# A landmark-attention stage with four 32-row score tiles in one PSUM buffer, half of its softmax tiles left unnormalised, and its residual loads ahead of the expert weights

## What is computed

```python
kernel1 = softmax(einsum('bhnd,bhmd->bhnm', Q, K_l), axis=-1)   # 16 heads, 64 landmarks
SV = matmul(matmul(kernel1, iterative_inv(kernel2)), matmul(kernel3, V))
out = SV @ w_proj                                                # added to the residual
```

## Time and profile before

| | us |
|---|---|
| median of 3 runs | 2002.76 (2001.23 to 2005.08) |
| the profiled execution | 2008.18 |
| its span in the trace | 2006.5 |
| kernel1 in it | 1517.05 to 1673.47 |

### The profile page before, as it was taken

One profiled execution on the slowest core, in us unless ns is written; L12 is line 12 of the kernel. 1 busy time (PEld: TensorE's weight loads), 2 busy tenths in 40 slices (PEclk: granted clock), 3 DMA queues, 4 the chain that ended last, 5 costly groups with the idle time before them and its releaser, 6 DMA issues. The chain is left out here.

```text
span 2006.5 us, 34424 instructions
## 1 busy us (share of the span) xinstructions
PE 1745.2 (87%) x11935; PEld 926.1 (46%) x12021; DVE 1530.2 (76%) x3643; ACT 1015.0 (51%) x1941; POOL 538.1 (27%) x623
## 2 busy tenths in 40 slices
PE   0898946889999999999999978978677888999998
PEld 0465621223232323232323235645575657888854
DVE  7997649988988989898999938678566994444456
ACT  3464422566767676767676835357413544232210
POOL 0343243000000000000151010045405884666610
PEclk9999976999999999999999988998787999999999
DMA  3466575005040505050551155122215224666566
GB/s 105 152 199 220 186 193 117 1 2 162 2 163 2 162 3 162 3 148 17 153 139 52 43 183 173 64 80 90 95 46 203 97 94 124 192 186 191 166 227 218
DMA packets 162940, 241.33 MB, mean 120 GB/s; under 512 B 21939, under 2 KB 131507, under 8 KB 161107
## 3 DMA queue, kind: packets, MB, share of 16 engines
q1 hardware_dynamic: 126930, 155.08, 25.9%
q0 software_dynamic: 23136, 75.65, 10.7%
q10 hardware_dynamic: 12704, 8.39, 1.4%
HBM read 118.86 MB, written 119.82 MB: 119 GB/s over the span
## 5 line engine op out<-in xcount | busy, mean ns | idle before, releaser
L1118 ACT ACTIVATE c_prob<-c_pst 128x512 f32<-128x512 f32 (+1 forms) x1152 | 578.8, 578 | 301.5 <-PE c_pst L1083 122.9
L1226 DVE TENSOR_REDUCE c_mx<-c_pf 128x2 f32<-128x1024 f32 x384 | 459.4, 1221 | 35.2 <-PE c_pf L1060 31.9
L1079 PE MATMUL c_pst<-c_qa,c_ka 128*128 128x512 bf16 (+3 forms) x1194 | 339.2, 355 | 14.4 <-DMA c_qa<-c_mT 5.8
L1095 PE MATMUL c_po<-c_prob,c_vh 128*32 128x512 f32 (+3 forms) x2560 | 295.7, 544 | 1.0 <-ACT c_prob L1118 0.4
L1060 PE MATMUL c_pf<-c_ka,c_qa 64*128 64x512 bf16 (+3 forms) x1280 | 230.1, 367 | 50.3 <-DMA c_ka<-s_kbias 22.5
L1222 DVE CUSTOM_DVE_ANT_0 c_spare<-c_pf,c_cut 128x384 f32<-128x384 f32 (+3 forms) x512 | 230.8, 491 | 28.6 <-PE c_pf L1060 24.3
L1079 PEld LDWEIGHTS c_pst<-c_qa,c_ka 128*128 128x128 bf16 x1280 | 110.2, 97 | 202.8 <-ACT c_prob L1118 110.1
L1060 PEld LDWEIGHTS c_pf<-c_ka,c_qa 64*128 64x128 bf16 x1280 | 59.4, 93 | 311.7 <-DVE c_mx L1226 122.2
L992 POOL IOTA c_zero<- 128x24 int32 x6 | 1.3, 214 | 632.3 <-PE c_po L1095 632.3
L2218 POOL DMA_INDIRECT s_parts<-x_yr,x_tags x144 | 140.4, 975 | 85.5 <-DVE x_yr L2867 62.8
L2852 DVE TENSOR_TENSOR x_h<-x_ps,x_sg 128x256 f32<-128x256 f32 x72 | 30.6, 425 | 142.0 <-ACT x_sg L2821 142.0
(11 more groups left out here) (440 smaller groups left out, 3027.1 us busy)
## 6 DMA issues: line engine op xcount, KB each, us to landing
s_slots<-c_zero POOLq DMA_DIRECT2D x6, 3264.0 KB, 17.0
x_xr<-s_slots SPq DMA_DIRECT2D x72, 272.0 KB, 2.8
x_rows<-s_parts SPq DMA_DIRECT2D x8, 2048.0 KB, 8.9
c_qa<-s_qs SPq DMA_DIRECT2D x64, 192.0 KB, 7.3
c_ka<-s_ks SPq DMA_DIRECT2D x64, 192.0 KB, 7.5
s_qs<-b_parts SPq DMA_DIRECT2D x32, 256.0 KB, 2.4
s_ks<-b_parts SPq DMA_DIRECT2D x32, 256.0 KB, 2.7
s_vs<-b_va SPq DMA_DIRECT2D x32, 256.0 KB, 3.8
```

Of the source, the lines that this page charges most:

```text
L1079: mm = nc.tensor.matmul(pst[:, u % NS, at:at + qn], ka[:, s, hh, kt * P:(kt + 1) * P], qa[:, s, hh, qb * QB + q0:qb * QB + q0 + qn], start ...
L1095: mm = nc.tensor.matmul(po[HV * h:HV * h + HV, q0:q0 + qn], vh[:, s, kt, h, :], prob[:, a % NP, h, at:at + qn], start=(kt == 0), stop=(a i ...
L1118: nc.scalar.activation(prob[:, g % NP, hh, 0:w], pst[:, u % NS, 0:w], ACT.Exp).then_inc(exp_ok, 1)
L1226: nc.vector.tensor_reduce(mx[:, fh:fh + 2, qt, part], pf[:, slot, :, 0:kn], AX.X, ALU.max).then_inc(max_ok, 1)
```

## The change

Scores. They are now made in four tiles of 32 rows (two heads each) instead of two of 64 rows, so a step takes 8 products of 128 columns instead of 4 of 256. The four tiles write four PSUM banks, half of each, and there is one such buffer instead of two: scores of step n wait for the shift of step n - 1. On TensorE scores move behind values in a round.

Odd steps (batch 1). Their exponentials are not summed on VectorE nor normalised on GpSimd. k_e is turned as it is, values multiplies it with W and, with 8 further products, with a tile of ones, which gives each head's sum on every one of that head's 16 rows. A new part on VectorE, invert, takes the reciprocal of those 128 x 256 sums (k_ss), and a new part on GpSimd, scale, multiplies k_svt with it before the projection. Even steps keep sums and normalise.

Loads. SP now issues one residual tile, then one piece of the weights, and so on, where the residual tile of step n waits for the add of step n - 2; all ten weight pieces stand behind the first ten residual tiles.

Start. Head mask and identity are kept from an earlier stage instead of being made again (in the experts stage too); each of the four kbd products signals by itself, and TensorE waits for w_proj only ahead of the first projection.

```diff
-    p1 = ps("k_p1", [P, 2, H, M])
+    p1 = ps("k_p1", [P, 4, 512])
+    in_banks = p1[:, :, 0:H // 4 * M].rearrange("p g (x m) -> p g x m", m=M)
...
-    pv = ps("k_pv", [P, K, P])
+    pv = ps("k_pv", [P, 2, K, P])
...
-            load_ahead(sp)
...
-            staggered(sp, N, DEPTH, [(6, load)])
+            def weights(n, u, s):
+                if n < WEIGHTS:
+                    load_weights(sp, n)
+
+            staggered(sp, N, 0, [(0, load), (0, weights)])
...
+            def scale(n, u, s):
+                if s == 1:
+                    wait(pool, ss_ok, u + 1)
+                    wait(pool, va_ok, n + 1)
+                    nc.gpsimd.tensor_tensor(svt[:, 1], svt[:, 1], ss[:], ALU.mult).then_inc(scaled_ok, 1)
+
+            staggered(pool, N, DEPTH, [(6, scale), (0, send), (3, normalise)])
...
-                wait(pe, d_ok, n - 1)
+                if n < B:
+                    pe.wait_ge(kbd_ok, (n + 1) * K)
+                wait(pe, d_ok, n)
                 for k in range(K):
...
+                    for g in range(4):
+                        rows = slice(32 * g, 32 * g + 32)
+                        mm = nc.tensor.matmul(p1[:, g, k * 2 * M:(k + 1) * 2 * M], QT[rows, s * K + k, u * P:(u + 1) * P],
+                                              kbd[rows, s * K + k, 2 * g:2 * g + 2, :].rearrange("p h m -> p (h m)"),
+                                              start=True, stop=True, tile_position=(32 * g, 0))
...
+                for part in range(1 + s):
+                    for k in range(K):
+                        for g in range(4):
+                            mm = nc.tensor.matmul(pv[32 * g:32 * g + 32, part, k, :], ones[:] if part else W[:, s * (H // 2) + k * 4 + g, :],
+                                                  et[:, s, g * K + k, :], start=True, stop=True, tile_position=(0, 32 * g))
...
+                if s == 1:
+                    wait(pe, scaled_ok, u + 1)
...
-            staggered(pe, N, DEPTH, [(5, turn), (1, scores), (6, output), (5, values)])
+            staggered(pe, N, DEPTH, [(5, turn), (6, output), (5, values), (1, scores)])
...
+            def invert(n, u, s):
+                if s == 1:
+                    wait(dve, va_ok, n + 1)
+
+                    wait(dve, scaled_ok, u)
+                    nc.vector.reciprocal(ss[:], pv[:, 1]).then_inc(ss_ok, 1)
...
-            staggered(dve, N, DEPTH, [(7, add), (2, shift), (3, sums)])
+            staggered(dve, N, DEPTH, [(7, add), (6, invert), (2, shift), (3, sums)])
```

More of the change, by code:

```diff
@@ L2476, in _ @@
             step = Steps(pool, chain_p)
[L2477 to L2482, removed]
+            step(nc.gpsimd.memset(ones[:], 0.0))
+            step(nc.gpsimd.memset(ones[0:M, 0:D], 1.0))
+            nc.gpsimd.memset(ones[M:P, D:2 * D], 1.0).then_inc(ones_ok, 1)
+            pool.wait_ge(ones_ok, 1)
             per = TOPK * NR // N
@@ L2509, in _ @@
         def _(pe):
-            pe.wait_ge(kbd_ok, 1)
-            pe.wait_ge(id_ok, 1)
-            pe.wait_ge(w_in, 16)
             def scores(n, u, s):
-                wait(pe, d_ok, n - 1)
+                if n < B:
+                    pe.wait_ge(kbd_ok, (n + 1) * K)
+                wait(pe, d_ok, n)
                 for k in range(K):
[L2518 to L2523, removed]
+                    for g in range(4):
[3 more added lines that the diff above has]
+                                              start=True, stop=True, tile_position=(32 * g, 0))
                 mm.then_inc(s_ok, 1)
             def turn(n, u, s):
-                wait(pe, n_ok, n + 1)
+                if s == 0:
+                    wait(pe, n_ok, u + 1)
+                else:
+                    wait(pe, e_ok, n + 1)
+                src = e[:, 1 + u % 2] if s else en
                 wait(pe, ta_ok, n)
                 for i in range(H // 2):
-                    mm = nc.tensor.transpose(pt[:, i, :], en[:, s, 2 * i:2 * i + 2, :].rearrange("p h m -> p (h m)"), ident[:])
+                    mm = nc.tensor.transpose(pt[:, i, :], src[:, 2 * i:2 * i + 2, :].rearrange("p h m -> p (h m)"), ident[:])
                 mm.then_inc(t_ok, 1)
@@ L2537, in values @@
                 wait(pe, va_ok, n)
[L2538 to L2542, removed]
+                wait(pe, ss_ok, n // 2)
+                if n == 1:
+                    pe.wait_ge(ones_ok, 1)
+                for part in range(1 + s):
[3 more added lines that the diff above has]
+                                                  et[:, s, g * K + k, :], start=True, stop=True, tile_position=(0, 32 * g))
                 mm.then_inc(v_ok, 1)
@@ L2564, in exp @@
                 wait(act, d_ok, n + 1)
-                wait(act, n_ok, n - 1)
-                nc.scalar.activation(e[:, s], d[:, s], ACT.Exp).then_inc(e_ok, 1)
+                if s == 0:
+                    wait(act, n_ok, u)
+                else:
+                    wait(act, t_ok, n - 3)
+                nc.scalar.activation(e[:, 1 + u % 2 if s else 0], d[:, s], ACT.Exp).then_inc(e_ok, 1)
             def take_values(n, u, s):
@@ L2617, in expert_weights, with load, experts @@
     w_in = nc.alloc_semaphore(name="x_w_in")
[L2619 to L2623, removed]
+    def load(eng, piece):
+        shared, kind = divmod(piece, 2 * (C // P) + 1)
+        e0, n, gs, us, ds = (E, NSH, sgw, suw, sdw) if shared else (0, E, gw, uw, dw)
+        k, up = divmod(kind, 2)
+        if kind == 2 * (C // P):
             eng.dma_start(d[:, e0:e0 + n, :], ds).then_inc(w_in, 16)
+        else:
+            eng.dma_start(gu[:, k, e0:e0 + n, up * I:(up + 1) * I], (us if up else gs)[k * P:(k + 1) * P]).then_inc(w_in, 16)
     return gu, d, w_in, load
-def experts(nc, turned_dram, gu, d, w_in, owner, y4_space, x2, slots_dram, parts_dram, out_dram, N, C, I, E, NSH,
+def experts(nc, turned_dram, gu, d, w_in, ident, owner, y4_space, x2, slots_dram, parts_dram, out_dram, N, C, I, E, NSH,
             TOPK, ctx):
```

63 lines of the change are left out of this document (31 added, 32 removed).

## The result

The changed kernel takes 2026.08 us (median of 4 runs, 2025.83 to 2030.6); the kernel before, with the runs taken beside it, 2003.92 us (4 runs). The ratio is 1.0116, 95% interval 1.0096 to 1.0136: slower by 22 us. The forecast was 2018.6 us, +15.8 us, with a range from 2004 to 2030. Runs of one kernel scatter by up to 15 us. In the traces of all kernels here the time outside this stage differs by up to 8 us, while a part of the stage that an edit leaves alone repeats within 0.1 us. So from here on I compare the stage's length in the traces, one trace for each kernel: from SP's first issue in it to SP's first load of the experts stage.

The account below looks back on a forecast made before the run. GpSimd was taken to set the pace, with VectorE 0.15 us per step behind; then VectorE's chain. Start -0.8, first pair +1.0, pairs +9.6, end +6.0 sum to +15.8 us: 2018.6 us from 2002.76, range 2004 to 2030 (own range 2010 to 2027).

Parts of the forecast that it names:

- The reciprocal: VectorE's new 128 x 256 reciprocal of an odd step's sums (k_ss): 1.77 us, continued from rows of 4 and 16 columns.
- Rivals 1 and 4: VectorE's new reciprocal: rival 1, 0.42 us, total 1997.0, chance 12%; rival 4, 2.3 us, total 2027, chance 5%.
- The chain: VectorE's queue with the reciprocal waiting for ScalarE's copy behind the exponential: 9.83 us per pair of steps, +9.6 us.
- The first pair: First of the 13 pairs: its reciprocal waits for doubled values at the slow clock, some +1.0 us.
- Rival 2: TensorE's clock falls as it idles from turn until scale: +0.9 x 13, total 2030; chance 8%.
- the cover: Single score buffer hidden: even step's scores done at 6.4 or 6.9 us, ahead of VectorE's maximum at 7.36.
- E: The end of the subtraction of a pair's even step on VectorE, from which the forecast counts times.
- The end: From E of step 30 to the last add: 22.15 us against 16.18, +6.0 us.
- The exchange: From the last add to the experts stage's first load; the forecast had no term for it.
- The start: From the stage's start to E of step 4: first maximum 3.5 us sooner, E of step 4 -0.8 us.
- The wait of the first add: VectorE's first add waits 7.06 us for its residual tile before the change; taken as gone.
- rival 3: Loads still hold add up, a residual tile queued behind the 2048 KB piece: +7 us, total 2026; chance 5%.

Follow-up runs that it names:

- e2: The changed kernel with a plain copy in place of the 128 x 256 reciprocal on VectorE; stage 152.05 us, median 2001.66 us, ratio 1.0000.
- e1: The changed kernel with ScalarE's copy of k_svt put ahead of the exponential; stage 161.35 us, median 2008.77 us, ratio 1.0032.
- e8: The changed kernel with three unread products on TensorE where it waits for scale of each odd step; stage 172.65 us, median 2025.70 us, ratio 1.0108.
- e3: The changed kernel with the scale of the last step alone on VectorE instead of GpSimd; stage 174.28 us, median 2020.59 us, ratio 1.0092.
- e4: The kernel before with the new order of loads alone; stage 151.65 us, median 2001.26 us, ratio 0.9987.
- e5: The kernel before with the new scores alone (four 32-row tiles, one buffer, behind values); stage 157.90 us, median 2005.72 us, ratio 1.0005.

## Why the prediction was right, and where its sizes were off

**The reciprocal.** Forecast 1.77 us by continuing two short rows, measured 1.757. From 16 to 256 columns it is (1757 - 253) / 240 = 6.27 ns per column, against 6.33 taken. The operation takes four times as long as the copy of its size in e2 (0.425 us). The 8.3 ns that I had estimated from the Trainium skill, page "VectorE: DVE Perf Modes", section "First, the fixed hardware budget", does not agree with the measured 6.27; that the section calls reciprocal an iterative division goes with a price above the copy's, though no run here shows its steps. Rivals 1 and 4 fall.

**The chain.** Forecast and shown by e1 and e2. Its period without disturbance is 9.55 us, forecast 9.83: I had counted the reciprocal's whole length, 1.77, where the next instruction starts 1.68 after it, 0.25 between k_rs and add where 0.17 was enough, and full spacings (1.25 and 0.34) where an instruction without a wait follows sooner (1.20 and 0.28). 13 x 0.28 = 3.6 us too much. The first pair was to cost 1.0 us more; it cost 0.4.

**The clock.** Rival 2, which I gave 8%, came true in part: granted 0.91 in much of the pairs and 0.87 in the end instead of 1.00. It costs 3.0 us in the pairs (e8), and not on the path that I had named. I had let it delay the odd step's values and the copy; VectorE's waits for the copy hardly changed, and instead three even maxima waited 2.1 us for scores. So the cover that I had given the single score buffer, scores done at 6.4 to 6.9 us against 7.36, went in those pairs: in the pair shown scores end 7.57 us after E. That 127.60 stands close to the forecast of 128.8 is luck: 3.6 us too much in the period and 0.6 in the first pair covered the 3.0 of the clock.

**The end.** The mis-sized term: +6.0 forecast, +8.4 measured. With the clock at 1.00 the end is 22.09 us (e8), where I had worked out 22.15; the 2.5 us more are the clock.

**The exchange.** A term that the sum lacks, +3.6 us. I looked at which engine does the last work of the stage, but not at what GpSimd does after its own last work. The DRAIN was in the trace before, 7.19 us long and hidden; the change moved GpSimd's last work to the end and so took its cover away. e3 gives it back.

**The start.** Forecast -0.8, measured 0.0: the four-tile scores at the slow clock took 1.24 us and not 1.08, which stands on the path three times ahead of step 4. That is 0.5 of the 0.8 us; the rest lies in signals and in the first scores, which start 1.39 us after SP's first issue and not 1.25. The wait of the first add did go, as assumed, and rival 3 did not come; its worth was 5.0 us (e4).

What the change does well is small beside this: the loads give 5.0 us, the start 2.4 with two score buffers and nothing with one (e5 loses 2.3). Its odd part relieves GpSimd of half its normalising, but gives VectorE, whose pace without waits is close to GpSimd's, more work than it takes away: 1.76 instead of 1.21 + 0.25 for the sums of an odd step. I had put the distance at 0.15 us per step; the five pairs at 8.16 (see e4) show that it is at least 0.29, so some 0.6 us per pair is what relieving GpSimd could give by these rows, before this extra work is paid. With the copy first a pair takes 8.67 (e1), hardly less than GpSimd's 8.74.

## What to carry to other kernels

Price an operation by rows of the same operation at two sizes, not by others of its size: 12 more columns in two short rows foretold a 1.76 us instruction within 1%. When a new instruction is put in a queue that is nearly full, look at what it waits for on the other engine and what stands ahead of that there; here one exchange of two entries in ScalarE's list was worth 16.8 us against a net loss of 21.4. And when the last work of a stage moves to another engine, look at what that engine still has to do before the stage may end.

## What the hardware showed that I had not expected

GpSimd's DRAIN at the end of this stage takes 5.84 us whether it begins at the end (after) or 11 us before VectorE's (e3), and 7.19 us in the kernel before; the other engines' take 0.1 to 1.6 us. All seven kernels with the odd part have the 5.84 and all four that normalise every step 7.19 or 7.20, wherever the DRAIN begins; what sets its length, no run here shows. And unneeded products made the stage faster: with TensorE idle for 2.2 us in each pair its granted clock was 0.91 over much of the pairs and single pairs lasted up to 10.5 us, while with three more products in that gap it was 1.00 and pairs lasted 9.55 (e8).
